# A decoder layer on one core: sums turned by a narrow 0/1 matrix, other turns in four strips, outputs in halves, another order at the opening and in the feed-forward

## The chip, the cores and the metric

The kernel runs on one core of a Trainium2 chip (trn2). The metric is the device time of one execution in microseconds; lower is better. The engines are called by the names of the profile: PE is TensorE (matmuls; PEld are its weight loads), DVE is VectorE, ACT is ScalarE, POOL is GpSimd and SP is SyncE, which issues all DMAs here.

## The reference

Four batches of 256 tokens, width 128, go through one pre-norm decoder layer:

```python
x = x + attn(layernorm(x), wq, wk, wv, wo)          # 2 heads of 64, rotary, causal
x = x + xattn(layernorm(x), ctx, ctx, Wq, Wk, Wv, Wo, bq, bk, bv, bo)   # 16 heads of 8, 1601 keys
x = x + ffn(layernorm(x), W1, b1, W2, b2, scale)    # hidden width 512, GELU
```

In the feed-forward, W1 and W2 get an addition per batch, `scale` times outer products of the normalized tokens 1 to 16. Nearly all the work is the cross-attention: 4 x 16 heads, 256 queries by 1601 keys, softmax over the keys, and sums of values of width 8. All tensors are float32.

## The kernel before

**Units and tiles.** The cross-attention is cut into 16 units: batch b, four heads each (`UNITS`, unit v is batch v // 4). A unit has 13 key tiles t (12 of 128 keys, one of 65). For each tile TensorE makes scores, keys by queries, for two pairs of heads (`scores`, L1195), each pair in one of three PSUM banks `score`; ScalarE takes the exponential of a bank, 128x512 (`exponential`, L998); TensorE then sums values by probabilities in `products` (L1177), four matmuls of 32 weights each, on four column strips of the array, three tiles behind the scores. A ninth value column of ones gives the sum of the probabilities. The profile counts a float32 matmul as two instructions, a transpose as one.

**Maxima.** The softmax needs each row's maximum before the scores. So TensorE makes the scores of unit v + 1 (and the first of v + 2) a first time, queries by keys, in 26 pieces ("M", `maximum`, L1211), and VectorE reduces each 128x512 piece (L785). GpSimd splits the negated maxima in three bf16 parts (L640 to L648). "mT" turns them: eight small transposes (`turn_max`, L1237), and ScalarE copies the three rows of each half of the partitions into `q_unit` (L1011), where they meet rows of ones in `k_unit` (`MR` = 3 rows, for both heads of a pair alike). Queries and keys are themselves split in bf16 parts, 48 rows, so that a score is a bf16 matmul of 51 rows.

**End of a unit.** "norm": ScalarE copies the sums (queries along the columns, L1009), TensorE turns them with two float32 transposes of 128x128 (`norm`, L1248), VectorE takes the reciprocals and scales (L798). In tile t = 4 of the next unit.

**Other steps.** "prep" items prepare the next batch: norms, xT (turn tokens, `turn_tokens`, L1255), qk and qks (self-attention projections with rotary), e0/e1 (energies), soft, pT0/pT1, v, av (L1299), wo, x2T, q, K0 to K3 (keys), parts0/parts1 (GpSimd splits the keys), store0/store1 (SyncE writes them to DRAM, from where `load_keys` fetches them), V0 to V3 (values). "post" items end a batch: OT, Wo, x3T, low (the additions), h0/h1 (hidden, with GELU on ScalarE) and out. The GELUs of batches 0 and 1 are done together in unit 11, tile 3 (`HIDDEN`), because ScalarE must load a table for GELU and another for the exponential. The outputs of batches 0 and 1 follow at (13, 8) and (15, 4) (`OUT_AT`: unit, tile), in one item of 64 matmul instructions each (L1404).

**Order.** There is no planner. One list, `PLAN`, is written out by hand: `start_plan` (the opening: `FIRST`, `BETWEEN`, the maxima of unit 0), `unit_plan(v)` for 16 units, and `end_plan`. Every engine runs through this same list and takes its own part of each item, in order, so the list is each engine's queue. `COUNT` and `COUNT_AT` say how many M pieces stand in each tile, `AHEAD` and `AHEAD_AT` how many of unit v are made before unit v - 1 begins, `SIDE` which side steps stand in which tile, `sums_due` which sums. Results of M, mT, norm, prep and post steps go through four PSUM banks `ring` in rotation (`take`): TensorE waits until the earlier use of a bank is drained. "keep" items are filler matmuls.

## Time and profile before

| | us |
|---|---|
| median of 3 runs | 377.39 |
| lowest, highest | 377.14, 378.44 |
| profiled execution, its own time | 377.22 |
| its span, first to last instruction | 375.4 |
| TensorE matmuls busy | 350.0 (93%) |
| VectorE busy | 297.1 (79%) |
| ScalarE busy | 296.4 (79%) |
| GpSimd busy | 123.5 (33%) |

A busy time is the time in which at least one instruction of the kind ran. A row of a timeline gives the start, the time until the last of the merged instructions ends, the engine, the line of the kernel, the operation, output and inputs with their shapes, and how many instructions it merges; `128*32 128x256` is a matmul with 128x32 weights and 256 columns. Matmuls are pipelined: two rows can overlap, and the distance between starts says what one costs. Units are told apart by ScalarE's copy of the sums, which ends them: unit 0 at 78.6, unit 10 at 269.8, unit 15 at 359.8. The opening lasts to 51.6, the end from 359.8 on.

### The profile page before, as it was taken

The page shows a single profiled execution, that of the slowest core. Times are in us where ns is not written, and L with a number is a line of the kernel's source. Part 1 is how long each engine was busy: PE and PEld are TensorE (multiplying, and loading weights), DVE is VectorE, ACT ScalarE, POOL GpSimd, SP SyncE. Part 2 cuts the span into 40 slices and gives each one's busy share as a digit, 9 for nine tenths or more (in the row PEclk, how much of TensorE's full clock was granted, in tenths as well). Part 3 has the DMA queues.
Part 4 walks back from the last instruction along what each step waited for, and adds up shares of the span by engine and source line. Part 5 has one row for each costly group of instructions (what it writes and reads, how often), then busy time and mean ns, then how long its engine had stood idle before and what let it go on. Part 6 is the DMA issues. An engine that isn't in the chain of part 4 may idle for free.

```text
span 375.4 us, 11889 instructions
## 1 busy us (share of the span) xinstructions
PE 350.0 (93%) x4819; PEld 163.1 (43%) x4819; DVE 297.1 (79%) x601; ACT 296.4 (79%) x598; POOL 123.5 (33%) x202
## 2 busy tenths in 40 slices
PE   7778899999999999999999999999999999999996
PEld 3332343544545444444534445434433434443455
DVE  3779978699998997699999987999977879780013
ACT  1653258989898789898897898898987999799762
POOL 3510746398020205799310133382000036000000
PEclk9999988999999999999999999999998999999999
DMA  7535495033420221135302022023020101000001
GB/s 246 199 107 154 158 274 181 2 135 129 120 84 2 99 95 56 58 131 179 129 27 78 2 79 58 3 63 134 13 69 2 63 19 58 17 2 3 16 2 30
DMA packets 20010, 30.72 MB, mean 82 GB/s; under 512 B 1432, under 2 KB 17218, under 8 KB 19956
## 3 DMA queue, kind: packets, MB, share of 16 engines
q1 hardware_dynamic: 19956, 29.97, 24.8%
q8 instruction: 38, 0.62, 0.7%
q14 instruction: 16, 0.13, 0.1%
HBM read 18.62 MB, written 11.34 MB: 80 GB/s over the span
## 4 chain that ended last, share of the span: by engine, by line
PE 58%; DVE 20%; POOL 10%; ACT 8%; issue 4%; DMA 1%; DVEq 0%; ACTq 0%; POOLq 0%
PE wsum L1191 19%; DVE part_max L785 15%; PE score L1205 13%; PE ring L1161 12%; PE ring L1227 6%; ACT probs L1004 4%; POOL k_parts L630 3%; POOL k_rest L670 2%; POOL k_parts L675 2%; PE score L1161 1%; PE ring L1244 1%; ACT q_unit L1015 1%; PE ring L1252 1%; PE ring L1258 1%; POOL xn L686 1%
## 5 line engine op out<-in xcount | busy, mean ns | idle before, releaser
L785 DVE TENSOR_REDUCE part_max<-ring 128x1 f32<-128x512 f32 x384 | 239.0, 683 | 27.1 <-PE ring L1227 25.3
L1004 ACT ACTIVATE probs<-score 128x512 f32<-128x512 f32 (+1 forms) x416 | 223.3, 597 | 31.3 <-PE score L1205 28.4
L1191 PE MATMUL wsum<-probs,v_aug 128*32 128x256 f32 (+1 forms) x1664 | 134.6, 392 | 3.0 <-ACT unit_ctx L1009 2.9
L1205 PE MATMUL score<-q_unit,k_unit 51*128 51x256 bf16 (+1 forms) x832 | 128.7, 275 | 4.1 <-ACT probs L1004 3.5
L1227 PE MATMUL ring<-k_unit,q_unit 51*128 51x512 bf16 x384 | 121.3, 387 | 3.1 <-DVE part_max L785 2.1
L1205 PEld LDWEIGHTS score<-q_unit,k_unit 51*128 51x128 bf16 (+1 forms) x832 | 48.8, 96 | 97.9 <-ACT probs L1004 57.6
L1191 PEld LDWEIGHTS wsum<-probs,v_aug 128*32 128x32 f32 (+1 forms) x1664 | 39.3, 109 | 39.5 <-issue 20.2
L1227 PEld LDWEIGHTS ring<-k_unit,q_unit 51*128 51x128 bf16 x384 | 35.2, 94 | 17.4 <-DVE part_max L785 9.2
L630 POOL TENSOR_TENSOR max_parts<-neg_max,c_sb 128x8 bf16<-128x8 f32 x16 | 3.4, 210 | 111.9 <-DVE neg_max L793 111.9
L802 DVE RECIPROCAL unit_rsum<-ring 128x8 f32<-128x8 f32 x16 | 3.2, 201 | 21.6 <-PE ring L1252 21.6
L1015 ACT ACTIVATE q_unit<-ring 3x512 bf16<-3x512 bf16 x32 | 18.6, 580 | 1.1 <-PE ring L1244 0.8
L1064 ACT ACTIVATE k_full<-ring,w_sb 128x401 f32<-128x401 f32 x15 | 9.0, 598 | 11.3 <-PE ring L1161 11.2
L709 POOL TENSOR_SCALAR prob_diag<-c_sb,prob_rsum 128x128 f32<-128x128 f32 x12 | 7.0, 603 | 29.8 <-DVE prob_rsum L896 29.8
L630 POOL TENSOR_TENSOR k_parts<-k_full,c_sb 128x802 bf16<-128x802 f32 x6 | 9.1, 1522 | 21.6 <-ACT k_full L1064 21.6
L1161 PE MATMUL ring<-ctx_sb,w_sb 128*32 128x401 f32 x128 | 14.2, 508 | 1.7 <-DVE part_max L785 0.8
L1161 PE MATMUL ring<-w_sb,ctx_sb 128*32 128x128 f32 (+1 forms) x408 | 14.8, 275 | 0.4 <-DVE part_max L785 0.4
L788 DVE TENSOR_REDUCE part_max<-ring 128x4 f32<-128x260 f32 x32 | 12.5, 424 | 1.9 <-PE ring L1233 1.7
L1161 PE MATMUL ring<-xn_t,w_sb 128*32 128x256 f32 x160 | 12.0, 410 | 1.0 <-ACT xn_t L1024 0.8
L721 POOL TENSOR_TENSOR var<-mv,c_sb 128x2 f32<-128x2 f32 x4 | 0.8, 194 | 36.4 <-DVE mv L933 36.4
L1161 PEld LDWEIGHTS ring<-w_sb,ctx_sb 128*32 128x32 f32 (+1 forms) x408 | 10.4, 108 | 4.3 <-issue 2.1
L1155 PE MATMUL score<-still 128*128 128x512 bf16 x27 | 9.7, 483 | 1.2 <-DVE still L757 1.2
L1075 ACT ACTIVATE v_aug<-ring 128x512 f32<-128x512 f32 (+1 forms) x15 | 7.7, 512 | 3.7 <-PE ring L1161 3.4
(137 smaller groups left out, 337.8 us busy)
## 6 DMA issues: line engine op xcount, KB each, us to landing
k_unit<-k_rows SPq DMA_DIRECT2D x30, 300.2 KB
ctx_sb<-ctx_t SPq DMA_DIRECT2D x3, 800.5 KB, 8.6
...
```

The costliest lines, as they stand in the source:

```text
L630: return g.tensor_tensor(to, src, C("zero").to_broadcast([P, src.shape[1]]), ALU.add)
L785: v_.tensor_reduce(part_max[:, par, q, head, hp, c:c + 1], ring[s][:, 0:MW], AX.X, ALU.max)\
L788: v_.tensor_reduce(part_max[:, par, :, head, :, MC], ring[s][:, 0:2 * QT * MREST].rearrange("p (q h c) -> p q h c", q=QT, h=2), AX.X, ALU. ...
L1004: a_.activation(probs[0:rows, i % PB, :], score[k % EB][0:rows, :], ACT.Exp)\
L1015: last = a_.activation(q_unit[rows, item[1] % UB, :, :].rearrange("p h n -> p (h n)"), ring[s][rows, 0:S].bitcast(BF16), ACT.Copy)
L1064: a_.activation(k_full[:, CW * c:CW * (c + 1)], ring[s][:, 0:CW], ACT.Identity, bias=W("bk"))\
L1075: last = a_.activation(v_aug[:, nb % 3, VT * t0:VT * (t0 + tn)] .rearrange("p (n c) -> p n c", c=VW)[:, :, 0:DX], ring[s][:, 0:D * tn].rea ...
L1155: mm(score[0][:, :], still[:, 0:P], still[:, :], start=True, stop=True)
L1161: last = mm(to[at:end, :], lhs_t[:, at:end], rhs, start=start, stop=stop)
L1191: last = mm(wsum[32 * j:32 * j + 32, 0:S], v_aug[0:rows, v // UB % 3, at:at + 32], probs[0:rows, i % PB, S * (j // 2):S * (j // 2 + 1)], s ...
L1205: last = mm(score[i % EB][0:keys, S * hp:S * (hp + 1)], k_unit[rows, u, L * hp + P * t:L * hp + P * t + keys], q_unit[rows, u, hp, :], sta ...
L1227: mm(ring[s][:, 0:MW], q_unit[rows, u, hp, P * q:P * (q + 1)], k_unit[rows, u, L * hp + MW * c:L * hp + MW * (c + 1)], start=True, stop=Tr ...
```

## The change

- The sums of a unit are turned by matmuls with a 0/1 matrix `heads` of 36 columns, in four strips of 32 weights, instead of two 128x128 transposes. Only the 9 used rows of each strip come out, so VectorE reads them at a step of 9 instead of 32.
- `turn_tokens` turns by matmuls with the identity, in strips. `av` is in strips of 32 instead of halves of 64.
- The maxima of a pair of heads are turned together: four transposes of 6 rows instead of eight of 3. `MR` is 6; each head of a pair has its own three rows of ones (and zeros in the other's), so the same six rows of maxima serve both. A score is a matmul of 54 rows; ScalarE's copy reads 256 columns and writes them twice. The rows of ones and the zeros that DMAs bring are six; the copy of k3 becomes two.
- Outputs of batches 0 and 1 are in halves, o0 and o1 (128 tokens each): at (11, 5), (11, 6), and (15, 2), (15, 7).
- The list changes: in `HIDDEN`, h1 of batch 1 comes earlier and one sums step goes to tile 4; in the opening, K2 of batch 1 goes before the last maxima of unit 0, qk before mT, K3, parts1 and store1 into unit 0 (tiles 0 and 2, `KEYS_AT`), and two of unit 1's M pieces into unit 0; v goes from tile 5 to tile 2, xT from tile 4 to 3.

The diff, without most of its unchanged lines:

```diff
@@ -49,12 +49,12 @@
 TR = TERMS * DX
-MR = 3
+MP = 3
+MR = 2 * MP
 VQ = 4 * VW
-TWO_ONES = np.array([0x3F803F80], np.uint32).view(np.float32)[0]
@@ -73,9 +73,9 @@
                         ("Wo", D), ("W1", HF), ("W2", FJ * D), ("b1", FJ), ("b2", D), ("scale", 1)])
-C_N = _columns(C_COLS, [("ident", P), ("pow", 2 * B), ("eps", QT), ("zero", 1), ("one_rows", 1),
+C_N = _columns(C_COLS, [("ident", P), ("pow", 2 * B), ("eps", QT), ("zero", 1), ("one_rows", 2),
                         ("cos", S), ("sin", S), ("mask_bf", 3 * P // 2),
-                        ("mask", 3 * P), ("pick", 3 * P), ("pick_keys", 3 * P), ("ones", L), ("zeros", S)])
+                        ("mask", 3 * P), ("heads", VQ), ("pick", 3 * P), ("pick_keys", 3 * P), ("ones", L), ("zeros", S)])
@@ -108,9 +108,16 @@
-    one_rows = np.zeros((P, 1), np.float32)
-    for par in range(2):
-        one_rows[HALF * par:HALF * par + MR] = 1.0
+    heads = np.zeros((P, VQ), np.float32)
+    for j in range(4):
+        heads[32 * j:32 * j + VW, VW * j:VW * (j + 1)] = np.eye(VW, dtype=np.float32)
+    put("heads", heads)
+    one_rows = np.zeros((P, 2), np.float32)
+    ones = np.zeros((MR, 2 * L), np.uint16)
+    for hp in range(2):
+        for par in range(2):
+            one_rows[HALF * par + MP * hp:HALF * par + MP * (hp + 1), hp] = 1.0
+        ones[MP * hp:MP * (hp + 1), L * hp:L * (hp + 1)] = 0x3F80
@@ -120,7 +127,7 @@
         put(name, pick.view(np.float32))
-    put("ones", np.full((MR, L), TWO_ONES, np.float32))
+    put("ones", ones.view(np.float32))
@@ -135,8 +142,8 @@
 SIDE = {
-    (3, 1): [("prep", "ln1", 2)], (3, 4): [("prep", "xT", 2)], (3, 7): [("prep", "qk", 2)], (3, 9): [("prep", "qks", 2), ("ctx", 3)],
-    (0, 1): [("prep", "e0", 1), ("prep", "e1", 1)], (0, 4): [("prep", "soft", 1)], (0, 5): [("prep", "v", 1)],
+    (3, 1): [("prep", "ln1", 2)], (3, 3): [("prep", "xT", 2)], (3, 7): [("prep", "qk", 2)], (3, 9): [("prep", "qks", 2), ("ctx", 3)],
+    (0, 1): [("prep", "e0", 1), ("prep", "e1", 1)], (0, 2): [("prep", "v", 1)], (0, 4): [("prep", "soft", 1)],
@@ -154,11 +161,12 @@
+KEYS_AT = {(0, 0): ("K3", "parts1"), (0, 2): ("store1",)}
 HIDDEN_AT = (11, 3)
-HIDDEN = (("post", "h0", 0), "M", "M", ("post", "h1", 0), ("post", "h0", 1), "M", "PV", "M", ("post", "h1", 1), "PV", "M",
-          "M", "PV")
-OUT_AT = {(13, 8): ("post", "out", 0), (15, 4): ("post", "out", 1)}
+HIDDEN = (("post", "h0", 0), "M", "M", ("post", "h1", 0), ("post", "h0", 1), "M", ("post", "h1", 1), "PV", "M", "M", "PV", "M")
+OUT_AT = {(11, 5): ("post", "o0", 0), (11, 6): ("post", "o1", 0), (15, 2): ("post", "o0", 1), (15, 7): ("post", "o1", 1)}
@@ -170,7 +178,7 @@
 BETWEEN = ((("k10", 0),), (("k11", 0),), (("k20", 0),), (("k21", 0), ("K0", 1)), (("K1", 1), ("parts0", 1)),
-           (("k3", 0), ("U4", 0)), (("U5", 0),), (("U6", 0),))
+           (("k3", 0), ("U4", 0)), (("U5", 0), ("U6", 0)), (("K2", 1),))
@@ -180,10 +188,10 @@
 AHEAD = (11, 11, 6, 8)
-AHEAD_AT = {1: 6, 13: 17, 14: 11, 15: 8}
+AHEAD_AT = {1: 4, 13: 17, 14: 11, 15: 8}
          (3, 2, 2, 2, 2, 2, 3, 2, 2, 2, 2, 2, 3), (2, 2, 2, 2, 2, 2, 2, 2, 2, 2, 2, 2, 2))
-COUNT_AT = {0: (2, 2, 2, 2, 2, 2, 2, 2, 2, 2, 2, 2, 2), 11: (2, 2, 2, 8, 4, 3, 2, 2, 2, 2, 1, 1, 1),
+COUNT_AT = {0: (2, 2, 2, 2, 2, 2, 3, 2, 2, 2, 2, 2, 3), 11: (2, 2, 2, 8, 4, 3, 2, 2, 2, 2, 1, 1, 1),
@@ -206,8 +214,9 @@
     g, h = KT * v + t, KT * HIDDEN_AT[0] + HIDDEN_AT[1]
-    due = range(g - 3, g) if g == h else () if g in (h + 1, h + 2) else range(g - 3, g - 2)
+    due = range(g - 3, g - 1) if g == h else (h - 1,) if g == h + 1 else () if g == h + 2 else range(g - 3, g - 2)
@@ -239,6 +248,7 @@
                 plan.append((*what, b + off))
+        plan += [("prep", name, 1) for name in KEYS_AT.get((v, t), ())]
@@ -254,9 +264,8 @@
     plan += [("M", 0, k) for k in range(3 * len(BETWEEN), MU)] + [("ctx", 2), ("prep", "store0", 1)]
-    plan += [("M", 1, k) for k in range(4)] + [("prep", "K2", 1), ("keep", 2), ("mT", 0), ("prep", "qk", 1)]
-    plan += [("M", 1, k) for k in range(4, ahead(1))] + [("prep", "qks", 1), ("prep", "K3", 1)]
-    return plan + [("prep", "parts1", 1), ("prep", "store1", 1), ("keep", 1)]
+    plan += [("M", 1, 0), ("M", 1, 1), ("prep", "qk", 1), ("mT", 0), ("M", 1, 2), ("prep", "qks", 1)]
+    return plan + [("M", 1, k) for k in range(3, ahead(1))]
@@ -398,7 +407,7 @@
         max_rest = sb("max_rest", [P, QT * 4])
-        max_parts = sb("max_parts", [P, QT * 4, 3], BF16)
+        max_parts = sb("max_parts", [P, QT * 4, MP], BF16)
@@ -595,7 +604,7 @@
                         sp.dma_start(out[item[2], P * q:P * (q + 1), :], y_out[:, item[2] % 2, q, :]).then_inc(y_free, 16)
-                elif kind == "post" and item[1] == "out":
+                elif kind == "post" and item[1] in ("out", "o1"):
@@ -798,7 +807,7 @@
                 s, n = take(item)
-                got = ring[s][:, 0:S].rearrange("p (q j c) -> p q j c", q=QT, j=4)
+                got = ring[s][:, 0:QT * VQ].rearrange("p (q j c) -> p q j c", q=QT, j=4)
@@ -968,6 +977,13 @@
                             .then_inc(last_y, 1)
+                elif name in ("o0", "o1"):
+                    dve.wait_ge(y_free, 16 * (pb // 2 * 2 + 1))
+                    dve.wait_ge(x2_b2_set, pb + 1)
+                    s, n = take(item)
+                    q = int(name[1])
+                    v_.tensor_tensor(y_out[:, pb % 2, q, :], ring[s][:, 0:D], x2_b2[:, pb % 3, q, :], ALU.add)\
+                        .then_inc(drained[s], 1)
@@ -1012,8 +1028,8 @@
                     rows = slice(HALF * par, HALF * par + MR)
-                    last = a_.activation(q_unit[rows, item[1] % UB, :, :].rearrange("p h n -> p (h n)"),
-                                         ring[s][rows, 0:S].bitcast(BF16), ACT.Copy)
+                    last = a_.activation(q_unit[rows, item[1] % UB, :, :],
+                                         ring[s][rows, 0:S // 2].bitcast(BF16).unsqueeze(1).to_broadcast([MR, 2, S]), ACT.Copy)
@@ -1089,12 +1105,14 @@
                     a_.activation(k_unit[:, 0, L * hp + MW * c:L * hp + MW * (c + 1)], ring[s][:, :], ACT.Identity,
-                                  bias=C("one_rows")).then_inc(drained[s], 1)
+                                  bias=C("one_rows")[:, hp:hp + 1]).then_inc(drained[s], 1)
                     s, n = take(item)
-                    a_.activation(k_unit[:, 0, :].rearrange("p (h n) -> p h n", h=2)[:, :, MW * MC:L],
-                                  ring[s][:, 0:2 * MREST].rearrange("p (h n) -> p h n", h=2), ACT.Identity,
-                                  bias=C("one_rows")).then_inc(drained[s], 1)
+                    for hp in range(2):
+                        last = a_.activation(k_unit[:, 0, L * hp + MW * MC:L * (hp + 1)],
+                                             ring[s][:, MREST * hp:MREST * (hp + 1)], ACT.Identity,
+                                             bias=C("one_rows")[:, hp:hp + 1])
+                    last.then_inc(drained[s], 1)
@@ -1238,24 +1256,23 @@
                 for par in range(2):
-                    for hp in range(2):
-                        for q in range(QT):
-                            at = S * hp + P * q
-                            last = turn(ring[s][HALF * par:HALF * par + MR, :].bitcast(BF16)[:, at:at + P],
-                                        max_parts[:, 4 * q + 2 * par + hp, :], ident_bf[:, :])
+                    for q in range(QT):
+                        last = turn(ring[s][HALF * par:HALF * par + MR, :].bitcast(BF16)[:, P * q:P * (q + 1)],
+                                    max_parts[:, 4 * q + 2 * par:4 * q + 2 * par + 2, :].rearrange("p h t -> p (h t)"),
+                                    ident_bf[:, :])
                 for q in range(QT):
-                    last = turn(ring[s][:, P * q:P * (q + 1)], unit_ctx[:, P * q:P * (q + 1)], C("ident"))
+                    last = strips(ring[s][:, VQ * q:VQ * (q + 1)], unit_ctx[:, P * q:P * (q + 1)], C("heads"))
                 for q in range(QT):
-                    last = turn(ring[s][:, P * q:P * (q + 1)], src[:, q, :], C("ident"))
+                    last = strips(ring[s][:, P * q:P * (q + 1)], src[:, q, :], C("ident"))
@@ -1299,10 +1316,9 @@
                     for q, k in ((1, 0), (1, 1), (0, 0)):
-                        for h in range(HA):
-                            last = mm(ring[s][DA * h:DA * (h + 1), P * q:P * (q + 1)],
-                                      v_self[:, k, DA * h:DA * (h + 1)],
-                                      prob_self_t[:, h, P * (q + k):P * (q + k + 1)], start=k == 0, stop=k == q)
+                        for at in range(0, D, 32):
+                            last = mm(ring[s][at:at + 32, P * q:P * (q + 1)], v_self[:, k, at:at + 32],
+                                      prob_self_t[:, at // DA, P * (q + k):P * (q + k + 1)], start=k == 0, stop=k == q)
@@ -1401,16 +1417,20 @@
                         .then_inc(filled[s], 1)
+                elif name in ("o0", "o1"):
+                    pe.wait_ge(low_done, 2 * pb + 2)
+                    pe.wait_ge(score_drained, BANKS["post", "h1", pb] + 1)
+                    s, q = take(item), int(name[1])
+                    for j in range(FJ):
+                        last = strips(ring[s][:, 0:D], hidden[:, pb % 2, j, P * q:P * (q + 1)],
+                                      w2_all[:, pb % 3, D * j:D * (j + 1)], start=j == 0, stop=j == FJ - 1)
+                    last.then_inc(filled[s], 1)
                     pe.wait_ge(low_done, 2 * pb + 2)
-                    if ("post", "h1", pb) in BANKS:
-                        pe.wait_ge(score_drained, BANKS["post", "h1", pb] + 1)
-                        s = take(item)
-                    else:
-                        for needed in ("h0", "h1"):
-                            slot, m = RING["post", needed, pb]
-                            pe.wait_ge(drained[slot], m + 1)
-                        s = take(item)
+                    for needed in ("h0", "h1"):
+                        slot, m = RING["post", needed, pb]
+                        pe.wait_ge(drained[slot], m + 1)
+                    s = take(item)
```

## Rows read from the trace of the kernel before

**Rows 1.** The page: engines, chain by engine, costliest groups (busy us, mean ns).
```profile
PE 350.0 (93%) x4819; PEld 163.1 (43%) x4819; DVE 297.1 (79%) x601; ACT 296.4 (79%) x598; POOL 123.5 (33%) x202
...
PE 58%; DVE 20%; POOL 10%; ACT 8%; issue 4%; DMA 1%; DVEq 0%; ACTq 0%; POOLq 0%
...
L1191 PE MATMUL wsum<-probs,v_aug 128*32 128x256 f32 (+1 forms) x1664 | 134.6, 392 | 3.0 <-ACT unit_ctx L1009 2.9
```
**Rows 2.** Stretches, units 2, 10, 11, 13: length, each engine's busy us, granted clock last.
```profile
98.00:117.40 19.40, 19.27 (x336) 10.26 (x333) 17.54 (x33) 17.66 (x36) 2.40 (x6) 1.00 0.23 75
252.90:269.80 16.90, 16.13 (x203) 6.64 (x200) 16.83 (x33) 15.33 (x31) 2.92 (x6) 1.00 0.23 81
269.80:294.40 24.60, 23.39 (x275) 9.17 (x271) 20.25 (x38) 20.87 (x40) 0.82 (x4) 0.93 0.10 31
...
311.60:329.60 18.00, 17.23 (x263) 8.08 (x260) 15.20 (x30) 15.15 (x30) 7.22 (x14) 1.00 0.05 13
```
**Rows 3.** The same view of the three stretches of low clock.
```profile
46.00:49.60 3.60, 3.60 (x32) 1.56 (x28) 1.02 (x3) 1.77 (x3) 0.21 (x1) 0.53 1.00 245
59.80:63.10 3.30, 3.30 (x38) 1.43 (x33) 2.53 (x5) 3.00 (x9) 0.21 (x1) 0.51 0.70 257
...
281.20:284.50 3.30, 3.30 (x28) 1.09 (x27) 3.21 (x7) 1.79 (x5) 0.00 (x0) 0.55 0.02 5
```
**Rows 4.** TensorE in order of time: two key tiles around a token turn.
```profile
163.79 0.28 PE L1205 MATMUL score<-q_unit,k_unit 51*128 51x256 bf16 x1
...
164.33 0.44 PE L1258 MATMUL ring<-c_sb,xn 128*128 128x128 f32 x2
164.69 0.64 PE L1191 MATMUL wsum<-probs,v_aug 128*32 128x256 f32 x8
165.27 0.28 PE L1205 MATMUL score<-q_unit,k_unit 51*128 51x256 bf16 x1
...
165.81 0.42 PE L1191 MATMUL wsum<-probs,v_aug 128*32 128x256 f32 x4
```
**Rows 5.** TensorE in order of time: sixteen strip matmuls, then sums.
```profile
76.12 0.65 PE L1161 MATMUL ring<-w_sb,attn_out_t 128*32 128x128 f32 x16
76.59 0.61 PE L1191 MATMUL wsum<-probs,v_aug 128*32 128x256 f32 x8
```
**Rows 6.** TensorE in order of time: maxima turned, then the next tile's scores.
```profile
207.05 0.33 PE L1244 MATMUL ring<-ident_bf,max_parts 128*3 128x128 bf16 x5
...
207.81 0.28 PE L1205 MATMUL score<-q_unit,k_unit 51*128 51x256 bf16 x1
```
**Rows 7.** The opening in order of time; in brackets the idle time before, and its end.
```profile
47.65 1.19 ACT L1015 ACTIVATE q_unit<-ring 3x512 bf16<-3x512 bf16 x2 [0.84 <-PE ring L1244]
49.45 0.69 DVE L825 TENSOR_TENSOR rope_a<-ring,c_sb 128x512 f32<-128x512 f32 x1 [2.58 <-PE ring L1161]
51.61 0.28 PE L1205 MATMUL score<-q_unit,k_unit 51*128 51x256 bf16 x1
56.49 4.87 DVE L785 TENSOR_REDUCE part_max<-ring 128x1 f32<-128x512 f32 x8
```
**Rows 8.** Unit 11 after the GELUs, in order of time.
```profile
277.24 1.28 ACT L1004 ACT_TABLE_LOAD   x1 [0.82 <-PE score L1205]
280.04 7.63 DVE L785 TENSOR_REDUCE part_max<-ring 128x1 f32<-128x512 f32 x12
```
**Rows 9.** Unit 15 around output 1, in order of time.
```profile
347.97 1.95 PE L1161 MATMUL ring<-w_all,hidden 128*32 128x128 f32 x64
349.74 0.61 PE L1191 MATMUL wsum<-probs,v_aug 128*32 128x256 f32 x8
350.77 8.16 ACT L1004 ACTIVATE probs<-score 128x512 f32<-128x512 f32 x16 [1.93 <-PE score L1205]
```
**Rows 10.** TensorE in order of time: a tile of unit 14 without maxima.
```profile
337.86 0.61 PE L1191 MATMUL wsum<-probs,v_aug 128*32 128x256 f32 x8
338.74 0.64 PE L1191 MATMUL wsum<-probs,v_aug 128*32 128x256 f32 x8
```

## The prediction

> **What bounds the kernel now.** I read the page's engine line and chain first, then each unit as a stretch, then the order of time inside one key tile, then the three stretches of low clock. TensorE's matmuls are busy 350.0 of 375.4 us, and 58% of the chain of waits is TensorE, 20% VectorE [rows 1]. By stretches the bound changes hands: in a middle unit TensorE is busy 19.27 of 19.40 us; in unit 10 VectorE is, 16.83 of 16.90, with TensorE at 16.13; in unit 13 TensorE again, 17.23 of 18.00, with VectorE and ScalarE near 15.2 [rows 2]. Three stretches of 3.3 to 3.6 us ran at 1.2 instead of 2.4 GHz: 46.0 to 49.6, 59.8 to 63.1 and 281.2 to 284.5, granted clock 0.51 to 0.55 [rows 3]. The first starts while TensorE waits for the first unit's maxima, the second after a stretch bound by VectorE, the third after the GELUs.
>
> **Turns and sums, part by part.** A key tile is a block of scores and maxima, 163.79 to 164.33 (0.54 us), and a block of sums, 164.69 to 165.27 (0.58 us). Between them stands a pair of turns of 128x128: 0.36 us [rows 4]. The same 256 columns as strips of 32 weights, with sums behind them, take 76.12 to 76.59 = 0.47 us [rows 5]. So:
> - Turning tokens (`turn_tokens`) in strips costs 0.47 - 0.36 = 0.11 us more. Twelve such pairs lie beside other work (three batches, four turns each): +1.3 us.
> - Sums turned with the 36 columns of `heads`: 72 columns instead of 256. At the strips' rate that is 0.47 x 72/256 = 0.13 us, if issue keeps up. Upper bound: sixteen matmuls at the spacing of the long run, 1.77 us/64 = 27.7 ns [rows 9], give 0.44 us, 0.08 more than now. For the low end speaks that the first four matmuls of a sums block, on four strips (the view ends at 166), together take 0.42 us, where one has 0.39 in the mean of its group: strips start almost at once [rows 1, 4]. I take 0.18, a gain of 0.18 x 15 = 2.7 us (bounds: +1.2 to -3.5).
> - A pair's maxima together: now eight small turns and a sums block take 207.05 to 207.81 = 0.76, so the turns 0.18; four cost 0.09. Fifteen times: -1.35 us [rows 6]. ScalarE's two copies stay 512 wide (1.19 us the pair) and only read six rows.
> - The product `av` in twelve strips instead of six halves streams the same columns: 0, bounded by 0.15 a batch either way, since the trace shows it only as halves.
>
> Together 1.3 - 2.7 - 1.35 = -2.75 us of TensorE. Where VectorE is the bound (three or four units like unit 10 of rows 2) it buys nothing, so I count -2.0.
>
> The Trainium skill ("TensorE: Matmul & The Clock Gate", Part 1, "Wait — 56ns, not 53.3ns?") says that matmuls never start closer than about 25 ns, however few their columns. By it the sixteen cannot take under 0.40 us, and the narrow matrix would lose 0.04 us a unit instead of gaining 0.18; the rows on strips starting together speak against it, and no row here has a 36-column matmul. "TensorEngine Tiling (Array Packing)", Key Properties, says that changing the tiling mode drains the array; the trace agrees: 256 columns take 0.58 us before scores and 0.47 before other strips [rows 4, 5].
>
> **Opening.** Today ScalarE copies the turned maxima of unit 0 from 47.65, and scores start only at 51.61, because qk, two maxima, qks, K3 and a filler stand between [rows 7]. In the new order K2 goes into the stretch before (where VectorE is the bound, so free), K3 into tile 0, two maxima into the unit, and qk runs while GpSimd splits the maxima. The turn then comes some 0.5 us earlier, the copies end near 48.2, and TensorE has only three maxima-sized pieces and qks left, about 1.6 us at full clock: scores at about 48.2, 3.4 us earlier. VectorE then limits: it idles 2.58 us before 49.45 and then works on, to a run of eight maxima at 56.49 to 61.36 [rows 7]. I estimate that 1.0 us of idle stays between its shorter pieces, so 1.6 is won, and two maxima (0.61 each, 4.87/8) fewer lie before tile 6: 1.6 + 1.2 = 2.8 us. Bounds: 1.0 (only the idle counts and half the clock loss stays) and 3.4. K3 and v (moved from tile 5 to tile 2) lie under VectorE there; uncovered they would cost 0.47 x 401/256 = 0.7 and 0.47. SyncE's store of K3's parts comes later in its queue, with nothing but later batches' work behind it.
>
> **Feed-forward of batches 0 and 1.** ScalarE ends its GELUs, waits 0.82 us for scores and only then loads its exponential table, at 277.24, 1.28 us [rows 8]. One sums block fewer stands before those scores, so the table comes 0.58 us sooner. The two halves of output 0 (0.89 us each) go into tiles 5 and 6, where TensorE waits for those exponentials: hidden, and the gap ahead of the third low stretch closes. That stretch costs half its 3.3 us, 1.65. But VectorE runs twelve maxima without a gap from 280.04 to 287.67 [rows 8] and gets two more additions, so I count 1.0 (0 to 2.0). Output 0 leaves unit 13: 347.97 to 349.74 is such an output's price, 1.77 us [rows 9]. TensorE is the bound there with 0.77 us to spare, the others with 2.8 [rows 2]: -1.6 (0.8 to 1.8).
>
> **Last unit.** Norm and output 1 stand together; ScalarE idles 1.93 us until 350.77 and then runs sixteen exponentials without a gap, 8.16 us [rows 9], so its idle was on the path. A half is 0.89 us, and two or three score banks of 0.51 us hide it. TensorE also has its sum to do (a tile without maxima takes 337.86 to 338.74 = 0.88 us [rows 10], thirteen of them 11.4, and output 1.77), so I count -1.2 (0 to 1.9). SyncE waits for the second half, then sends both: one DMA as now.
>
> **Ends.** On the bare path a token pair's columns take 0.43 instead of 0.21 us: +0.2 at the first xT, the first x2T and the last x3T. The last sums' turn gets some 0.1 shorter. k3's second copy is under VectorE's maxima. Net +0.5. The first rows of ones double (6 instead of 3), but only unit 1's maxima need them.
>
> **Sum.** -2.0 - 2.8 - 1.0 - 1.6 - 1.2 + 0.5 = -8.1. The profiled execution took 377.22 us (span 375.4 and 1.8 around it), 0.17 under the median 377.39. Forecast: 377.2 - 8.1 = 369.1 us.
>
> **Rivals.**
> - *The second low stretch goes too.* Its 3.3 us at half speed cost 1.65; the earlier v and K3 fill the thin stretch ahead of it. Against: VectorE still limits that stretch. With narrow turns at the column rate (0.5 more): 367.0.
> - *VectorE takes over.* Its unbroken runs of twelve and eight maxima [rows 7, 8] leave nothing of the 1.0 in unit 11 and 1.0 of the 2.8 in the opening: 369.1 + 1.0 + 1.8 = 371.9.
> - *Narrow matmuls are held by issue*, 27.7 ns each: +1.2 instead of -2.7, three quarters of it felt: +2.9, so 372.0. This is what the skill's 25 ns would do, nearly.
> - *Slower: weight loads of strips are not hidden.* Place: the 27 turns beside other work (15 of sums, 12 of tokens), sixteen load-and-matmul pairs each. Without these two terms the change gains 1.0 (maxima turns) + 2.8 + 1.0 + 1.6 + 1.2 - 0.5 = 7.1 us; that is used up when a turn costs 7.1/27 = 0.26 over its 0.36, at 0.62/16 = 39 ns a pair. At 50 ns: 27 x 0.44 = 11.9, so 377.2 - 7.1 + 11.9 = 382. For it: a 36-column matmul has little time to hide a load. Against: pairs of 128 columns keep 27.7 ns.
>
> **How the numbers follow.** Chances: forecast 0.42, second stretch gone 0.20, VectorE 0.18, issue 0.12, slower 0.05; 0.03 for several gains failing at once, within 0.3% (1.1 us, about what a measurement here tells from no change). Hence faster 0.92, same 0.03, slower 0.05. Range: 365.5 (the first rival with the good ends of two terms) to 373.5 (VectorE and issue together, less 1.3 for the last unit's good end).
>
> **What would show it.** Norm: from its first matmul to the sums block behind it 0.13 to 0.2 us; 0.36 or more refutes it. Token turns 0.47, maxima turns 0.09. First scores near 48.2, low stretches at 46 and 281 gone, the one at 60 perhaps there. Last unit: no idle of ScalarE over 0.5 us. The forecast is wrong if unit 0 ends no more than 1 us sooner, or if units 1 to 7 are no shorter each: they should lose 0.15 us.

## The result and the profile after

| | before | changed |
|---|---|---|
| median of 6 runs each, us | 377.40 | 373.71 |
| lowest, highest | 376.26, 379.18 | 372.89, 374.80 |
| profiled execution, its span | 375.4 | 373.0 |
| mean granted clock of the profiled execution | 0.986 | 0.995 |

The ratio is 0.990, with a 95% interval of 0.987 to 0.993: faster by 1.0%, 3.7 us. The forecast was 369.1, with a range up to 373.5. The direction was right, the gain less than half of what was expected, and the time just outside the range.

The page of the changed kernel, with the lines that answer to [rows 1]:

```profile
PE 341.6 (92%) x5244; PEld 161.9 (43%) x5248; DVE 296.3 (79%) x603; ACT 297.8 (80%) x599; POOL 123.6 (33%) x202
...
PE 53%; DVE 20%; ACT 9%; POOL 8%; issue 5%; DMA 3%; SPq 2%; DVEq 0%; ACTq 0%; POOLq 0%
...
L1209 PE MATMUL wsum<-probs,v_aug 128*32 128x256 f32 (+1 forms) x1664 | 132.3, 386 | 1.8 <-ACT unit_ctx L1025 1.8
```

TensorE is busy 8.4 us less, the span is 2.4 us shorter. A part of the 8.4 is the clock, since work takes longer at the low clock and the trace before has three such stretches, this one one. So the work did go; most of the time it took did not.

The same stretches as in [rows 2], changed kernel: a low-clock stretch that stands earlier than any of [rows 3], then units 11, 13 and 15 (length, then busy time of each engine, then the granted clock):

```profile
24.20:27.60 3.40, 3.40 (x58) 2.74 (x52) 2.62 (x7) 1.46 (x4) 0.00 (x0) 0.54 0.01 2
...
269.51:294.22 24.71, 23.24 (x350) 10.52 (x345) 20.55 (x40) 20.85 (x40) 0.82 (x4) 1.00 0.11 36
...
311.27:327.33 16.06, 15.17 (x211) 6.15 (x206) 14.63 (x29) 15.20 (x31) 7.25 (x14) 1.00 0.02 4
...
344.08:356.60 12.52, 12.18 (x192) 5.25 (x190) 0.78 (x4) 10.73 (x22) 0.00 (x0) 1.00 0.04 12
```

The ends of the units (ScalarE's copy of the sums) give the account of the two profiled executions, in us against before: opening with units 0 and 1 -1.92; units 2 to 5 +0.26; unit 6 +1.35; units 7 to 10 +0.03; unit 11 +0.08; unit 12 -0.10; unit 13 -1.97; unit 14 +0.18; unit 15 -1.16; the end +0.83. That is -2.42. Unit 13 is as forecast. Unit 15 looks so too, but half of output 1 now counts in unit 14 (see out_only). The first units gained less, nothing was won from unit 2 to unit 12, and 1.35 us were lost in a place that the prediction does not mention.

**The sizes of the turns.** TensorE of the changed kernel in order of time: a norm, maxima turned, tokens turned:

```profile
179.06 0.34 PE L1179 MATMUL ring<-c_sb,unit_ctx 128*32 128x36 f32 x16
179.22 0.61 PE L1209 MATMUL wsum<-probs,v_aug 128*32 128x256 f32 x8
...
189.83 0.22 PE L1260 MATMUL ring<-ident_bf,max_parts 128*6 128x128 bf16 x2
...
190.47 0.30 PE L1223 MATMUL score<-q_unit,k_unit 54*65 54x256 bf16 x1
...
196.28 0.65 PE L1179 MATMUL ring<-c_sb,xn 128*32 128x128 f32 x16
196.74 0.61 PE L1209 MATMUL wsum<-probs,v_aug 128*32 128x256 f32 x8
```

From start to start the norm takes 0.16 us (forecast 0.18), maxima and sums together 0.64 instead of 0.76 [rows 6] (0.12 less, forecast 0.09), tokens 0.46 (forecast 0.47). The rival "held by issue" is dead: sixteen matmul instructions on four strips went by at 10 ns each, which is one in 40 ns on any one strip. The Trainium skill ("TensorE: Matmul & The Clock Gate", Part 1, "Wait — 56ns, not 53.3ns?") has 25 ns as the least; the measurement decides, for narrow matmuls on different strips. The durations were right, then, and what they were worth was wrong.

### The profile page after: what moved, and what is told of

It is laid out like the page before. It is cut to its first block, busy times and chain, and to the rows that moved or that the text cites. A ratio compares the mean times of both kernels' runs of the same rounds, so it can differ in the third digit from the quotient of the medians.

```text
span 373.0 us, 12750 instructions
## 1 busy us (share of the span) xinstructions
PE 341.6 (92%) x5244; PEld 161.9 (43%) x5248; DVE 296.3 (79%) x603; ACT 297.8 (80%) x599; POOL 123.6 (33%) x202
## 4 chain that ended last, share of the span: by engine, by line
PE 53%; DVE 20%; ACT 9%; POOL 8%; issue 5%; DMA 3%; SPq 2%; DVEq 0%; ACTq 0%; POOLq 0%
PE wsum L1209 17%; DVE part_max L794 15%; PE ring L1179 13%; PE score L1223 12%; PE ring L1245 6%; ACT probs L1020 5%; POOL k_parts L639 2%; DMA q_unit<-consts 2%; PE score L1179 1%; POOL k_rest L679 1%; POOL k_parts L684 1%; ACT q_unit L1031 1%; ACT prob_self L1067 1%; DVE energy L858 1%; ACT k_full L1080 1%
## 5 line engine op out<-in xcount | busy, mean ns | idle before, releaser
L1209 PE MATMUL wsum<-probs,v_aug 128*32 128x256 f32 (+1 forms) x1664 | 132.3, 386 | 1.8 <-ACT unit_ctx L1025 1.8
L1223 PE MATMUL score<-q_unit,k_unit 54*128 54x256 bf16 (+1 forms) x832 | 127.0, 273 | 7.2 <-ACT probs L1020 6.2
L1245 PE MATMUL ring<-k_unit,q_unit 54*128 54x512 bf16 x384 | 120.7, 383 | 6.2 <-DVE part_max L794 3.3
L1223 PEld LDWEIGHTS score<-q_unit,k_unit 54*128 54x128 bf16 (+1 forms) x832 | 48.2, 96 | 100.1 <-ACT probs L1020 54.2
L1245 PEld LDWEIGHTS ring<-k_unit,q_unit 54*128 54x128 bf16 x384 | 34.8, 93 | 19.9 <-DVE part_max L794 11.6
L1031 ACT ACTIVATE q_unit<-ring 6x512 bf16<-6x512 bf16 x32 | 18.6, 580 | 3.1 <-PE ring L1260 2.8
L1179 PE MATMUL ring<-w_sb,ctx_sb 128*32 128x128 f32 (+1 forms) x408 | 15.9, 292 | 0.6 <-DVE part_max L794 0.6
L1179 PEld LDWEIGHTS ring<-w_sb,ctx_sb 128*32 128x32 f32 (+1 forms) x408 | 11.6, 115 | 4.2 <-DVE part_max L794 2.0
L985 DVE TENSOR_TENSOR y_out<-ring,x_b 128x128 f32<-128x128 f32 x4 | 1.1, 287 | 12.8 <-PE ring L1179 12.8
L684 POOL TENSOR_TENSOR k_parts<-k_rest,k_parts 128x802 bf16<-128x802 f32 x6 | 10.3, 1712 | 0.5
```

The costliest lines, as they stand in the source:

```text
L684: g.tensor_tensor(k_parts[:, 2, cols], k_rest[:, cols], k_parts[:, 1, cols], ALU.subtract)\
L1031: last = a_.activation(q_unit[rows, item[1] % UB, :, :], ring[s][rows, 0:S // 2].bitcast(BF16).unsqueeze(1).to_broadcast([MR, 2, S]), ACT. ...
L1179: last = mm(to[at:end, :], lhs_t[:, at:end], rhs, start=start, stop=stop)
L1209: last = mm(wsum[32 * j:32 * j + 32, 0:S], v_aug[0:rows, v // UB % 3, at:at + 32], probs[0:rows, i % PB, S * (j // 2):S * (j // 2 + 1)], s ...
L1223: last = mm(score[i % EB][0:keys, S * hp:S * (hp + 1)], k_unit[rows, u, L * hp + P * t:L * hp + P * t + keys], q_unit[rows, u, hp, :], sta ...
L1245: mm(ring[s][:, 0:MW], q_unit[rows, u, hp, P * q:P * (q + 1)], k_unit[rows, u, L * hp + MW * c:L * hp + MW * (c + 1)], start=True, stop=Tr ...
```

## The experiments

A kernel's runs differ more than its parts do, and the mean granted clock tells why. In 91 executions of the kernel before, taken beside the experiments, the median span is 373.4 us at clock 0.995 (8 executions), 375.1 at 0.991 (30), 376.1 at 0.986 (28) and 376.9 at 0.982 (19). One step of 0.0045 is one stretch like those of [rows 3], 3.3 to 3.6 us at half clock. A straight line through all executions of all kernels, with one slope for all and a height for each, gives 1.03 us a step (plus or minus 0.11). The heights are the spans at full clock, and the table compares them. Four of 234 executions are left out as far off: one of norm_only (clock 0.938), one of later8 (509.9 us) and two of before_keep (455.2 us at clock 0.657, and 1026.0 us). The medians count them.

| kernel | median us | ratio to before (95%) | mean clock | against before at full clock, us |
|---|---|---|---|---|
| before | 377.7 to 378.4 | 1 | 0.987 | 0 |
| norm_only | 377.30 | 0.9986 (0.9951 to 1.002) | 0.987 | -0.7 ± 0.5 |
| pair_only | 376.82 | 0.9977 (0.9943 to 1.001) | 0.987 | -0.8 ± 0.5 |
| tok_only | 378.33 | 1.0038 (1.0004 to 1.0072) | 0.986 | +0.8 ± 0.5 |
| open_only | 376.73 | 0.9966 (0.9933 to 0.9998) | 0.995 | +0.5 ± 0.5 |
| out_only | 376.26 | 0.9961 (0.9939 to 0.9983) | 0.991 | -1.1 ± 0.5 |
| changed kernel, 6 runs | 373.71 | 0.9896 (0.9867 to 0.9926) | 0.997 | -1.8 ± 0.7 |
| changed kernel, 6 others | 373.86 | 0.9887 (0.9858 to 0.9916) | 0.997 | -1.8 ± 0.7 |
| later8 | 374.35 | 0.9919 (0.9890 to 0.9947) | 0.995 | -1.9 ± 0.6 |
| after_oldopen | 374.58 | 0.9935 (0.9907 to 0.9962) | 0.993 | -1.8 ± 0.6 |
| after_tokturn | 373.12 | 0.9893 (0.9865 to 0.9921) | 0.997 | -2.7 ± 0.7 |
| tok_early | 373.00 | 0.9860 (0.9816 to 0.9903) | 0.997 | -2.5 ± 0.7 |
| tok_keep | 372.52 | 0.9840 (0.9799 to 0.9880) | 0.998 | -2.9 ± 0.7 |
| tok_early_keep | 373.41 | 0.9857 (0.9814 to 0.9900) | 0.999 | -2.0 ± 0.8 |
| tok_late_out | 377.41 | 0.9967 (0.9930 to 1.0004) | 0.992 | +0.3 ± 0.5 |
| before_keep | 376.84 | 0.9967 (0.9931 to 1.0004) | 0.995 | +0.3 ± 0.6 |
| tok_keep2 | 371.99 | 0.9841 (0.9811 to 0.9870) | 0.999 | -3.1 ± 0.7 |

The five parts add up: -0.7 - 0.8 + 0.8 + 0.5 - 1.1 = -1.3 at full clock (changed kernel: -1.8 ± 0.7). Their low stretches add up only roughly: 2.9 an execution before, 1.8 fewer with the new opening and 0.9 fewer with the outputs in halves would leave 0.2; 0.6 to 0.8 were left. So of the some 4 us by which the means differ, 2.2 to 2.3 are the clock (2.1 to 2.3 steps of 1.03) and 1.8 the rest.

### One part each

norm_only, the kernel before with

```diff
-last = turn(ring[s][:, P * q:P * (q + 1)], unit_ctx[:, P * q:P * (q + 1)], C("ident"))
+last = strips(ring[s][:, VQ * q:VQ * (q + 1)], unit_ctx[:, P * q:P * (q + 1)], C("heads"))
```

> The kernel before with one part: each unit's sums turned with the 36 columns of heads. Size theory (the prediction's term): 0.18 us a unit on TensorE, of which three quarters is felt, 2.0 us in all. Cover theory: TensorE gets the 0.2 us back in each unit, but in a unit VectorE or ScalarE or a transfer is what the next scores wait for, so that the turn measures 0.16 us and the kernel gains 0 to 0.8 us. If units 1 to 5 (TensorE busiest) are 0.1 us or more shorter each and units 7 to 10 are not, the cover theory holds and says where.

Measured: -0.7 ± 0.5. The cover theory holds, but with other units than it named. The view by stretches of norm_only, units 2, 9, 12 and 13:

```profile
97.03:116.47 19.44, 19.09 (x349) 10.18 (x347) 17.56 (x33) 17.70 (x36) 2.41 (x6) 1.00 0.23 74
...
234.75:252.13 17.38, 16.58 (x230) 7.29 (x225) 17.31 (x33) 15.96 (x33) 10.43 (x21) 1.00 0.11 31
...
292.44:309.36 16.92, 16.15 (x231) 6.74 (x224) 13.91 (x30) 15.84 (x32) 4.01 (x9) 1.00 0.25 75
...
309.36:327.16 17.80, 17.03 (x279) 8.00 (x274) 15.24 (x30) 15.20 (x31) 7.25 (x14) 1.00 0.04 11
```

and the same units of the kernel before:

```profile
97.96:117.36 19.40, 19.27 (x336) 10.24 (x333) 17.58 (x33) 17.66 (x35) 2.40 (x6) 1.00 0.23 76
...
235.50:252.88 17.38, 16.78 (x216) 7.42 (x211) 17.31 (x33) 15.92 (x33) 10.42 (x21) 1.00 0.13 31
...
294.42:311.57 17.15, 16.38 (x217) 6.80 (x210) 13.93 (x30) 15.83 (x33) 4.00 (x9) 1.00 0.23 71
...
311.57:329.60 18.03, 17.26 (x265) 8.08 (x260) 15.23 (x30) 15.18 (x30) 7.22 (x14) 1.00 0.05 13
```

TensorE's busy time falls by 0.18 to 0.23 us in each. Units 12 and 13 are 0.23 us shorter, and so are 14 and 15; units 2 and 9 are not shorter at all. The chain of waits of norm_only, first microseconds of unit 2, shows what holds it:

```profile
98.26 0.43 PE wsum L1195 x8
98.69 0.21 PE score L1209
98.91 0.12 PE ring L1231
99.05 1.29 DVE part_max L789 x2
100.34 0.13 DVE unit_rsum L806
100.49 0.29 DVE x_ctx L809 x2
100.78 1.21 DVE part_max L789 x2
102.03 1.08 PE ring L1165 x32
```

VectorE reads the turned sums between its maxima, and TensorE then waits 0.21 us, until 102.03, for the ring slot that it frees; before there is no such wait. In seven units of the first ten (1, 2, 4, 5, 6, 8 and 9) TensorE's waits for VectorE's maxima grow by 0.1 to 0.2 us. (Units 3 and 7 had nothing to win: their turn stands next to a token turn, and there it takes 0.27 us in both kernels.) A unit with 19.27 of 19.40 us of TensorE looks bound by TensorE, yet at its head its maxima keep VectorE's pace. From unit 12 on VectorE has few maxima left (13.9 of 17 us), and only there a microsecond of TensorE is a microsecond.

pair_only:

```diff
-for hp in range(2):
-    for q in range(QT):
-        last = turn(... max_parts[:, 4 * q + 2 * par + hp, :], ident_bf[:, :])
+for q in range(QT):
+    last = turn(... max_parts[:, 4 * q + 2 * par:4 * q + 2 * par + 2, :]..., ident_bf[:, :])
```

> The kernel before with one part: the maxima of a pair of heads turned together, four small turns a unit instead of eight, six rows copied instead of three. Size theory: 0.09 us a unit, 1.0 us in all. Cover theory: 0 to 0.5 us. Rival: reading six partitions instead of three or filling k_unit's last columns with two copies costs the opening 0.1 to 0.3 us, so the whole is within 0.3 us of before.

Measured: -0.8 ± 0.5. Its trace has unit 1 0.11 and unit 14 0.19 us shorter, unit 2 0.35 longer, and the others from 3 to 15 the same within 0.1. So the trace shows 0.3 at most, which is the cover theory; where the runs have the rest from stays open.

tok_only:

```diff
-last = turn(ring[s][:, P * q:P * (q + 1)], src[:, q, :], C("ident"))
+last = strips(ring[s][:, P * q:P * (q + 1)], src[:, q, :], C("ident"))
```

> The kernel before with one part: tokens turned in strips, and the product av in strips of 32 rows. Prediction's term: 0.11 us more for each of twelve pairs beside other work (+1.0 felt) and +0.2 at each of three bare places: +1.3 to +1.6 us. Cover theory: the hidden ones cost nothing, only the bare ones in the opening and the tail, +0.4 to +0.7. Rival: the two-pass strips are faster than the full-tile turn on the bare path, 0 or a gain.

Measured: +0.8 ± 0.5, and 0.9 the other way when it is taken out of the changed kernel (below). By its one trace half of the price is at the bare ends (VectorE's first maximum 0.44 later, the end 0.41 longer), and units 1, 3, 5, 7 and 12 are 0.15 to 0.29 longer. So neither theory is right alone, and the runs show less than the trace.

open_only: the lists of the opening alone (`SIDE`, `KEYS_AT`, `BETWEEN`, `AHEAD_AT`, `COUNT_AT`, `start_plan`).

> The kernel before with one part: the new order of the opening. Prediction's term: -2.8 us. By the trace of the changed kernel unit 0 ends 1.4 us sooner and unit 5 still 1.7 us sooner, so -1.4 to -1.9 at unit 5; rival theory: unit 6 gives about 1.3 of it back, since the first maxima of unit 8 wait for loads whose time is set by a chain on GpSimd and the queues, and the end is then only 0.3 to 0.6 us sooner. If unit 6 is as long as before and the end is 1.5 us or more sooner, the loads are not what took it back.

Its profiled execution had no low stretch at all and took 2.8 us less. At the end of unit 1 it stood at -2.68; unit 6 gave nothing back, but units 2, 3, 4, 7 and 8 gave back 0.15 to 0.24 each, together 1.05, and unit 11 gained 1.22 because its low stretch was gone. And it was one of the two best of twelve executions. The mean of them is 1.4 us under before: 1.9 by the clock and +0.5 ± 0.5 at full clock. So loads did not take the gain back in this kernel, and the gain was the clock's.

out_only: `HIDDEN`, `sums_due`, `OUT_AT` and the items o0 and o1.

> The kernel before with one part: outputs of batches 0 and 1 in halves, batch 0's in unit 11, and the feed-forward's order. Prediction's terms: -1.0 in unit 11, -1.6 in unit 13, -1.2 in unit 15, -3.8 in all. Rival by the changed kernel's trace: unit 11 stays as long (the two halves stand in TensorE's order ahead of scores that ScalarE waits for, and what the earlier table load and the lost low stretch give back pays for them), so -2.0 from unit 13, -1.2 from unit 15 and 0 from unit 11: -3.0 to -3.2, and mostly at equal clock.

Measured: -1.1 ± 0.5 at full clock, and 0.9 low stretches fewer. Its trace has unit 11 at 24.70 us (before 24.63), unit 13 1.74 shorter, unit 15 0.96 shorter and unit 14 0.54 longer. The rival for unit 11 holds. The sum is under both forecasts, because the last unit did not gain its 1.2. Unit 14 is longer for a plain reason, TensorE in order of time:

```profile
344.67 1.08 PE L1168 MATMUL ring<-w_all,hidden 128*32 128x128 f32 x32
345.56 0.62 PE L1198 MATMUL wsum<-probs,v_aug 65*32 65x256 f32 x8
```

Half of output 1, at (15, 2), stands ahead of unit 14's last sums, so 0.89 us of it fall on unit 14's side of the border. Units 14 and 15 together are 0.42 us shorter. TensorE is busy 29.19 of their 29.83 us, so it bounds them, and the halves take no work from it. At full clock the trace gives +1.29 in unit 11 (24.70 against 23.41, see below), -1.74 and -0.42: -0.87, which agrees with the runs.

### Parts of the changed kernel undone or moved

after_oldopen: the changed kernel with the old lists of the opening.

> The changed kernel with the opening in the old order. Clock theory: the new opening costs 0.6 us at equal clock and takes away about 1.7 low-clock stretches of 1.06 us each; with the old one the mean granted clock falls by 0.005 to 0.008 and the time rises by 1.0 to 1.3 us over the changed kernel. Rival, the prediction's: 2.8 us slower than the changed kernel at any clock.

Measured: median +0.9 over the changed kernel, clock 0.993 instead of 0.997 (a little less of a fall than expected), the same span at full clock (-1.8 both) instead of 0.6 less. The prediction's 2.8 us are out.

after_tokturn: tokens turned as before.

> The changed kernel with tokens turned as before, by full-tile turns. If the strips of the token turns cost 0.9 us in the changed kernel as they did alone, it is 0.7 to 1.0 us faster than the changed kernel, 4.4 to 4.7 under before. Rival: the strips' cost there is hidden by other waits, 0 to 0.3 us.

Measured: 0.9 less at full clock, 0.6 to 0.7 in the medians. By the two traces the place is the end (and two bare turns of the opening). The chain of waits of the changed kernel there:

```profile
358.03 0.65 PE ring L1179 x16
358.67 0.97 PE score L1173 x4
...
363.58 0.65 PE ring L1179 x16
364.23 1.98 PE ring L1397 x16
```

and of after_tokturn:

```profile
357.15 0.44 PE ring L1275 x2
357.59 0.86 PE score L1173 x4
...
362.71 0.44 PE ring L1275 x2
363.14 1.79 PE ring L1397 x16
```

Each bare turn costs 0.21 us more, and what follows it 0.11 and 0.19. The prediction listed one bare turn at the end (x3T); the chain holds two, the first being the turn of the last batch's cross-attention result. The end is 16.4 us in the changed kernel, 15.6 here and before.

later8: the first maxima of unit 8 begin a tile later.

```diff
-AHEAD_AT = {1: 4, 13: 17, 14: 11, 15: 8}
+AHEAD_AT = {1: 4, 8: 8, 13: 17, 14: 11, 15: 8}
+COUNT_AT: 6: (2,) * 13, 7: (2, 2, 2, 3, 2, 2, 3, 2, 2, 2, 3, 2, 2)
```

> The changed kernel, but the first maxima of unit 8 that run ahead of it are eight instead of eleven, so that they begin a tile later in unit 6. Load theory: unit 6 loses the wait of 1.1 us for the loads of unit 8 and is 0.8 to 1.2 us shorter; the kernel gains 0.5 to 1.1 us if nothing later takes it. Rival: VectorE, which runs the maxima of units 7 and 8, then has more left in unit 7 and gives it back: 0, or up to 0.5 slower.

Measured: no gain at full clock. Unit 6 is 1.16 us shorter than in the changed kernel, unit 7 1.0 longer: VectorE, the rival. The wait that was moved is this one (TensorE of the changed kernel in order of time; in brackets the idle time before and what ended it):

```profile
185.75 0.39 PE L1245 MATMUL ring<-k_unit,q_unit 54*128 54x512 bf16 x1 [1.08 <-DMA q_unit<-consts]
```

The first maxima of unit 8 wait for its queries and zeros, loads that SyncE issues from 175.2 to 179.3. They hang on GpSimd's splitting of the queries, which GpSimd ends at 172.5 after 20 us without a gap, and on a store. TensorE came 1.7 us earlier than before at unit 5, the chain 1.1 (first of these loads 176.28 before, 175.20 now).

tok_early: on the base of after_tokturn, the keys' loads go ahead of the wait for the split queries.

```diff
+if b:
+    load_keys(b, 0)
 sp.wait_ge(q_split, 4 * (b + 1))
...
-    load_keys(b, 0)
     load_queries(b, 0)
```

> The changed kernel with full-tile turns of tokens (the base of these four), and SyncE issues the loads of the keys of units 4, 8 and 12 before it waits for the split queries, instead of behind their store. Load theory: the loads of unit 8 land 1 to 2 us sooner, the wait of 0.7 to 1.1 us in unit 6 goes, and the kernel is 0.6 to 1.0 us under its base (base 370.4 us of span at full clock). Rival: the queries' store now stands behind the keys' loads in the queue and lands later, so the queries take the keys' place as the late ones: no gain or up to 1 us slower. Second rival: the wait goes and VectorE, busy 17.9 of 18.7 us in unit 7, keeps the time: 0 to 0.3.

Measured: unit 6 0.8 us shorter than in the base, the whole 0.2 ± 1 longer at full clock. The loss in unit 6 differs from run to run anyway: 1.35 us in the changed kernel's first trace and 0.09 in its second, 1.0 in after_tokturn, 0.0 in tok_keep, 0.64 in tok_keep2. It is a race between TensorE and a queue; the mean price of these five, 0.6 us, is under what these runs tell apart.

tok_late_out: the same base, output 0 further back in unit 11.

```diff
-OUT_AT = {(11, 5): ("post", "o0", 0), (11, 6): ("post", "o1", 0), ...
+OUT_AT = {(11, 9): ("post", "o0", 0), (11, 11): ("post", "o1", 0), ...
```

> The same base, and the halves of output 0 stand in tiles 9 and 11 of unit 11 instead of 5 and 6. Cover theory (the prediction's: an idle TensorE hides them where it waits for ScalarE after the GELUs): farther back there is no such wait, unit 11 gets 1 to 2 us longer. Rival theory: they are not hidden in 5 and 6 either, since they stand in order ahead of scores and ScalarE idles 1.5 and 1.1 us there: unit 11 is as long within 0.3 us.

Unit 11 is 24.4 us, 0.3 shorter than in the base: the cover theory falls. What it would have hidden under is used up in the changed kernel, ScalarE in order of time, unit 11:

```profile
276.19 1.28 ACT L1020 ACT_TABLE_LOAD   x1 [0.94 <-PE score L1223]
277.49 2.19 ACT L1020 ACTIVATE probs<-score 128x512 f32<-128x512 f32 x4
281.22 1.09 ACT L1020 ACTIVATE probs<-score 128x512 f32<-128x512 f32 x2 [1.54 <-PE score L1223]
283.45 4.42 ACT L1020 ACTIVATE probs<-score 128x512 f32<-128x512 f32 x8 [1.14 <-PE score L1223]
```

The table is loaded 0.77 us sooner than in [rows 8], counted from the start of the unit (forecast 0.58); then ScalarE idles 1.54 and 1.14 us while TensorE makes the halves (279.69 and 281.48, 1.08 each).

The kernel as a whole lost 2.9 ± 0.8 us at full clock against its base, which neither theory expected. SyncE of tok_late_out in order of time:

```profile
288.95 0.42 SPq L610 DMA_DIRECT2D out<-y_out  x1
289.42 1.46 SPq L531 DMA_DIRECT2D k_unit<-k_rows  x2
```

and TensorE:

```profile
298.28 0.39 PE L1245 MATMUL ring<-k_unit,q_unit 54*128 54x512 bf16 x1 [2.09 <-DMA q_unit<-consts]
```

SyncE waits for o1 with the loads of the next units behind it in its queue. They start at 289.4 (in the changed kernel at 283.5), and unit 12 is 20.8 us instead of 16.9, with a low stretch behind the wait of 2.09 us. It is the queue that an output is moved past that prices the move.

### The clock

tok_keep, on the same base: five fillers in the idle time ahead of x2T.

```diff
-("k01", 0), ("ln2", 0), ("x2T", 0),
+("k01", 0), ("keep", 5), ("ln2", 0), ("x2T", 0),
```

> The same base, and five matmuls of the filler kind (0.21 us each) in TensorE's idle 1.6 us of the opening, 21.3 to 22.9 us, ahead of the low-clock stretch at 24 to 27.6. Clock theory: that stretch goes, the mean granted clock of the runs rises to 0.998 or more (base 0.997), and by 1.0 us a stretch the mean falls by 0.3 to 0.7 us. Rival: the clock falls for another reason (by the run, not by the idle time): same clock and same time.

tok_early_keep: both edits.

> The same base with both: keys' loads before the queries' wait, and the five fillers. If both theories hold, 0.9 to 1.7 us under the base: a median near 371.7 us; if both rivals hold, as the base, 373.1.

Measured: the stretch at 24 us is in neither trace, mean clock 0.998 and 0.999 (base 0.997), median 0.6 us less in tok_keep. That alone shows little: tok_early, without fillers, has no stretch at 24 us either, and six executions of each do not tell 0.6 us apart. tok_early_keep has the better clock and yet 373.41. Its traced execution was 1.8 us late already at VectorE's first maximum (30.39 against 28.60 in tok_keep), ahead of the loads that the edit moves, so nothing shows that these loads cost or gain anything.

before_keep: the kernel before, seven fillers between its last maxima; the order stays.

```diff
-plan += [("M", 1, k) for k in range(4)] + ...
+plan += [("M", 1, k) for k in range(2)] + [("keep", 1)] + [("M", 1, 2), ("keep", 1), ("M", 1, 3), ("keep", 1)] + ...
```

(and one each behind the last four groups of unit 0's maxima).

> The kernel before with seven filler matmuls (0.21 us each) between the last maxima of its opening, about 41 to 46 us, where TensorE waits for VectorE; the order of the opening stays the old one. Clock theory (the new opening gains by the granted clock alone, 1.0 to 1.2 us a low stretch): the stretch that begins at 46 us goes in most runs, the mean of the runs falls by 0.8 to 1.2 us against before, at equal clock 0. Rival (the new order gains by itself, since scores start 3.6 us sooner): the fillers bring 0 to 0.3 us, or cost what they take, up to 0.5.

Measured: mean clock 0.995 instead of 0.987, as much as the new opening brings, median 1.4 us less (its ratio's interval just reaches 1), mean of ten executions 1.6 less, and +0.3 ± 0.6 at full clock. Six of its ten executions have clock 1.000, none of the 91 of the kernel before. The clock theory holds. The two stretches of its trace that answer to [rows 3]:

```profile
42.00:46.00 4.00, 3.72 (x24) 1.37 (x24) 3.97 (x10) 0.27 (x1) 3.76 (x5) 1.00 0.39 151
46.00:50.00 4.00, 3.80 (x53) 1.79 (x56) 2.46 (x6) 1.77 (x3) 0.22 (x2) 1.00 0.98 241
```

Without the fillers TensorE was busy 2.85 of the 4 us from 42 to 46, and from 46 to 48 the clock was 0.50. The idle time before a stretch is what makes the fall likely, and fillers close it as well as another order does. At clock 1.000 the medians of the two can be compared as they are: 373.05 us of span in six executions of the old order with fillers, 372.85 in four of the new order (open_only).

after_again and tok_keep2 (tok_keep with five more fillers between the last maxima), on one chip:

> The changed kernel again, beside the others on one chip. If the granted clock is what differs from run to run, its span at full clock is 371.3 us again and its ratio to before 0.987 to 0.992. Rival: the runs so far were few, and it lies 1 us away at the same clock.

> The best version so far (the changed kernel with full-tile turns of tokens and five fillers at 21.3 us), with five more fillers between the last maxima of the opening. If fillers close the idle that comes before the low stretches, its mean clock is 0.999 or more and its median 371.8 to 372.5 us, 1.0 to 1.8 us under the changed kernel on the same chip. Rival: the fillers delay the last maxima and it is 0.3 to 0.6 us slower than with the first five alone (372.5).

Measured: the changed kernel is the same again (373.86; at full clock -1.8). tok_keep2 is the best version, 371.99 (371.47 to 373.06), 1.9 us under the changed kernel and 1.6% under before.

## Why the prediction failed, by its own steps

**Opening, -2.8: the step that failed most.** "Scores at about 48.2, 3.4 us earlier" was right in its distance: from VectorE's first maximum to the first score it is 23.2 us before and 19.6 after (20.8 with a low stretch between). The step behind it, "so 1.6 is won, and two maxima ... fewer lie before tile 6: 1.6 + 1.2", was not. From that first maximum to the end of unit 0 the old order takes 49.6 to 50.2 us with two low stretches' worth, 48.9 to 49.2 with one and 48.6 with none (before_keep); the new one 48.8 to 48.9 with one and 47.6 to 47.9 with none. At equal clock that is 0.1 to 1.0 us by the traces, and nothing by the runs. From its first score to its end unit 0 grew from 25.9 us (without a low stretch) to 28.0 and more, here before_keep and open_only:

```profile
51.15:77.07 25.92, 24.10 (x345) 11.64 (x344) 21.53 (x43) 22.97 (x51) 16.31 (x17) 1.00 0.37 128
...
48.28:76.43 28.15, 24.96 (x355) 11.75 (x351) 23.79 (x46) 23.53 (x50) 16.98 (x17) 1.00 0.47 141
```

Of the 2.23 us, 0.86 are work of TensorE that came in (K3, one more piece of maxima) and was to lie under VectorE; 1.37 are waits. From the first maximum to the end of unit 0 VectorE is busy 41.8 us in both: the pieces that were moved are still on its way. The chain of waits in the changed kernel shows where TensorE stands:

```profile
53.86 0.42 DVE neg_rowmax L863
54.28 0.59 DVE neg_rowmax L864
54.87 0.61 DVE part_max L794
...
56.88 1.09 ACT probs L1020 x2
57.96 1.74 ACT prob_self L1067 x8
59.70 0.49 ACT probs L1020
...
60.24 0.28 PE score L1223
```

Scores that start early run into the self-attention of batch 1, whose row maxima VectorE and whose exponentials (four, in eight instructions) ScalarE does in its turn. TensorE stands 1.11 us before 55.53 and 1.21 before 60.24; in the old order the wait at those exponentials is 0.15. The prediction looked at VectorE's idle time and at no chain behind it. What the new opening does give is 1.8 low stretches fewer, 1.9 us, which the prediction did not set apart from the order's own gain.

Unit 0 is not the whole account. Against before_keep, open_only is 0.67 us shorter to the end of unit 0 and 0.50 in unit 1, and gives back 1.03 in units 2, 3, 4, 7 and 8. In units 4 and 8 the wait of TensorE for ScalarE's exponentials grows from 0.36 to 0.90 us; v stands at tile 2 there instead of tile 5, which is the likely reason, though no run moves v alone. The steps of `SIDE` move for every batch, and the prediction priced them in unit 0 alone.

**Turns and sums, -2.0.** The sizes (-2.7, -1.35, +1.3) were right within 0.03 us a turn. "Three or four units like unit 10" where it buys nothing were eleven: in the traces the narrow turn paid in units 12 to 15, 4 x 0.23 us. The prediction's own sign came: "units 1 to 7 are no shorter", of which 2 to 7 lie between 0.04 shorter and 1.35 longer. The three parts together: -0.7 ± 0.9 at full clock.

**Unit 11, -1.0: missed.** The low stretch at 281 went and the table came sooner; "hidden" was wrong. norm_only had no such stretch either, and its unit 11 is 23.4 us: at full clock the halves cost 24.7 - 23.4 = 1.3 us there.

**Output 0 out of unit 13, -1.6: held.** -1.74 in out_only (-1.97 in the changed kernel, with the narrow turn's 0.23).

**Last unit, -1.2: missed.** Units 14 and 15 together gained 0.42 in out_only. ScalarE's longest idle there did shrink, from 1.93 to 0.76 us, but the prediction took it to be on the path, and TensorE bounds these units. The -1.16 of the changed kernel's unit 15 is nearly the sum of out_only's -0.96 and the narrow turn's -0.24, and the -0.96 is paid for in part by the +0.54 of unit 14.

**Ends, +0.5: too small.** Measured +0.83 at the end alone, with a second bare turn that the prediction left out, and some 0.4 at the two of the opening (tok_only).

**Not in the prediction: unit 6, 0 to +1.35.** None of the rivals was a transfer that comes too late. "VectorE takes over" (371.9) comes nearest to what happened: its mechanism works in most of units 1 to 11, not just in the opening and unit 11 as it was priced. The first rival, that the stretch at 60 goes too, came true and was worth 1.0 us, more than paid for by the rest. The strips' weight loads are hidden, as forecast.

**The range.** Its upper end was added up wrongly. "VectorE and issue together" is 369.1 + 2.8 + 2.9 = 374.8, and the last unit's good end (1.9) lies 0.7 under its term of 1.2, not 1.3: by the prediction's own terms that is 374.1, and 373.71 lies under it. That would not have saved the account, since issue cost nothing.

Open remains the last few tenths of the new order at full clock: the fit says +0.5 ± 0.5, the executions at clock 1.000 say -0.2. The changed kernel's -1.8 is more than the -1.3 of the five parts; the intervals allow for it.
